# Where layer 1's first operands are loaded inside the expert loop of a two-layer gated cross-attention network

## The reference

```python
x = x + tanh(g_xattn[0]) * L0_xattn(ctx_768, layernorm(x), mask, ...)   # 4 heads of 64, keys: context and x
x = x + tanh(g_ffn[0])   * L0_ffn(layernorm(x), ...)                    # 64 experts, grouped routing
x = x + tanh(g_xattn[1]) * L1_xattn(layernorm(x), ctx_768, ...)         # 16 heads of 64 over 77 keys
x = x + tanh(g_ffn[1])   * L1_ffn(layernorm(x), ...)                    # fake-quantised, 704 wide
```

```python
up   = einsum('td,edh->teh', xt, Wup) + bup
gate = einsum('td,edh->teh', xt, Wgate) + bgate
h    = silu(up) * gate * fs[:, :, None]          # fs: the routing shares
out  = einsum('teh,ehd->td', h, Wdown) + fs @ bdown
```

## Time and profile before

| | us |
|---|---|
| Median of 3 runs | 2242.48 |
| Lowest and highest | 2239.87, 2250.66 |
| The profiled execution | 2242.07 |
| Its span (first to last instruction) | 2240.00 |
| PE busy, x14922 | 2029.5 (91%) |
| DVE busy | 1682.1 (75%) |
| ACT busy | 1221.4 (55%) |
| POOL busy | 661.8 (30%) |

### The profile page before, as it was taken

How to read it: one execution, slowest core, us unless ns; L and a number is a source line. 1 busy time by engine, 2 the same in 40 slices (tenths; PEclk the granted TensorE clock), 3 DMA queues, 4 the chain that set the end, 5 groups by cost and what they waited for, 6 DMA issues and landing times.

```text
span 2240.0 us, 39247 instructions
## 1 busy us (share of the span) xinstructions
PE 2029.5 (91%) x14922; PEld 1248.5 (56%) x14922; DVE 1682.1 (75%) x2822; ACT 1221.4 (55%) x2885; POOL 661.8 (30%) x520
## 2 busy tenths in 40 slices
PE   7797889888977899999989999999999988899896
PEld 3454555555545444444456666666666656676643
DVE  5888686776879889977067777777778867676697
ACT  2455876858855666555523333333333367677585
POOL 0305877868767542000000000000000013243353
PEclk6898999999987999999999999999999999999997
DMA  4232000000000466454586666766766670000002
GB/s 120 70 107 61 1 2 1 2 1 3 21 20 1 164 228 240 200 216 175 210 237 197 203 190 200 205 189 195 205 190 204 192 212 16 1 1 2 1 1 75
DMA packets 134331, 255.34 MB, mean 114 GB/s; under 512 B 17868, under 2 KB 62785, under 8 KB 134017
## 3 DMA queue, kind: packets, MB, share of 16 engines
q1 hardware_dynamic: 113616, 185.05, 27.5%
q10 hardware_dynamic: 20529, 67.79, 7.7%
HBM read 169.28 MB, written 82.44 MB: 112 GB/s over the span
## 4 chain that ended last, share of the span: by engine, by line
PE 59%; DVE 21%; ACT 11%; POOL 4%; issue 3%; DMA 1%; SPq 1%; ACTq 0%; DVEq 0%; POOLq 0%
PE ps L519 56%; DVE arena L1042 8%; DVE arena L1051 6%; ACT arena L2006 5%; DVE arena L1045 3%; PE ps L527 3%; ACT arena L1756 3%; DVE arena L1048 2%; POOL arena L2111 2%; POOL arena L2072 1%; ACT arena L2014 1%; DVE arena L1058 1%; SPq L2205 1%; POOL arena L2124 1%; DMA arena<-share_scratch 1%
## 5 line engine op out<-in xcount | busy, mean ns | idle before, releaser
L519 PE MATMUL ps<-arena 128*128 128x512 f16 (+13 forms) x13708 | 1907.4, 297 | 135.1 <-DVE arena L1051 26.5
L519 PEld LDWEIGHTS ps<-arena 128*128 128x128 f16 (+7 forms) x13708 | 1109.9, 102 | 849.3 <-issue 115.6
L1042 DVE TENSOR_TENSOR arena<-arena 128x512 f32<-128x512 f32 (+6 forms) x992 | 715.1, 753 | 145.2 <-ACT arena L1964 92.4
L1756 ACT ACTIVATE arena<-ps,arena 128x512 f32<-128x512 f32 (+3 forms) x512 | 342.3, 686 | 178.0 <-PE ps L519 161.8
L1042 DVE TENSOR_TENSOR arena<-ps,arena 128x512 f16<-128x512 f32 (+11 forms) x440 | 238.8, 568 | 240.4 <-ACT arena L1760 87.2
L2072 POOL TENSOR_TENSOR arena<-arena 128x4 f32<-128x4 f32 (+5 forms) x51 | 85.2, 1672 | 1084.4 <-DVE arena L1045 1083.9
L1964 ACT CAST arena<-arena 128x512 f16<-128x512 f32 x256 | 158.2, 618 | 436.7 <-DVE arena L1042 432.2
L2111 POOL TENSOR_TENSOR arena<-arena 128x512 f16<-128x512 f32 (+1 forms) x288 | 350.8, 1240 | 65.0 <-ACT arena L1756 63.5
L1756 ACT ACTIVATE arena<-ps 128x512 f16<-128x512 f32 (+1 forms) x512 | 275.2, 611 | 89.2 <-PE ps L519 85.1
L1051 DVE TENSOR_REDUCE arena<-ps 128x1 f32<-128x1024 f32 (+5 forms) x246 | 224.5, 919 | 45.7 <-PE ps L519 42.9
L527 PE MATMUL ps<-arena 128*128 128x128 f32 (+4 forms) x1214 | 192.1, 286 | 70.7 <-DVE arena L1042 26.8
(11 more groups left out here) (81 smaller groups left out, 451.7 us busy)
## 6 DMA issues: line engine op xcount, KB each, us to landing
wide_scratch<-arena ACTq DMA_DIRECT2D x128, 512.0 KB, 2.6
arena<-share_scratch SPq DMA_DIRECT2D x512, 128.0 KB, 3.7
arena<-wide_scratch SPq DMA_DIRECT2D x128, 512.0 KB, 4.8
mq_scratch<-arena SPq DMA_DIRECT2D x16, 308.0 KB
vw_scratch<-arena SPq DMA_DIRECT2D x32, 154.0 KB
arena<-mq_scratch SPq DMA_DIRECT2D x16, 308.0 KB, 5.6
arena<-vw_scratch SPq DMA_DIRECT2D x8, 576.0 KB, 6.4
arena<-in_x SPq DMA_DIRECT2D x4, 1024.0 KB, 9.8
```

The lines of the kernel that those rows point to most:

```text
L519: return e.matmul(o, l, r, start=start, stop=stop, skip_group_check=True)
L1042: return e.tensor_tensor(o, a, b, op)
L1756: return e.activation(o, i, f, bias=bias, scale=scale)
```

## The change

The eight loads of `load1(0)` are no longer issued in a row in the pass of unit 10. `load1` gets an index and issues one load; the pass of unit 128 issues the first, those of units 136, 144, ... 184 the others, each behind the unit's share loads (and reloads, of which an even unit has none). The order of the eight is the same: 308, 308, 576 and 40 KB, and the same again. The waits for `fl` and `st` move along to unit 128. Batches 1 to 3 are loaded after the loop as before, all eight in a row.

```diff
-        def load1(b):
-            for n in range(2):
-                for k in range(2):
-                    load("op%d" % b, MQ[b][:, n, k, :], MQD[n, k, :, b, :])
+        def load1(b, i):
+            n, k = divmod(i, 4)
+            if k < 2:
+                load("op%d" % b, MQ[b][:, n, k, :], MQD[n, k, :, b, :])
+            elif k == 2:
                 load("op%d" % b, VW[b][:, n, 0:9, :], VWD[n, b, 0:1152, :].rearrange("(c p) d -> p c d", p=128))
+            else:
                 load("op%d" % b, VW[b][0:80, n, 9, :], VWD[n, b, 1152:1232, :])
...
-            if n == 10:
+            if n == 128:
                 W.wait_ge("fl", 8)
                 for z in range(3):
                     W.wait_ge("st%d" % z, 256)
-                load1(0)
+            if n >= 128 and n % 8 == 0 and n < 192:
+                load1(0, (n - 128) // 8)
...
         for b in range(1, 4):
-            load1(b)
+            for i in range(8):
+                load1(b, i)
```

## The result

| | before | after |
|---|---|---|
| Median, us (20 runs each) | 2241.64 | 2234.44 |
| Lowest and highest | 2232.36, 2253.62 | 2224.38, 2245.23 |
| Ratio after to before | | 0.9963, 95% interval 0.9947 to 0.9980 |
| The profiled execution | 2242.07 | 2245.03 |
| Its span | 2240.00 | 2243.3 |

What follows compares the result with a forecast made beforehand. TensorE (PE) was taken to bound the kernel, busy 91% of the span. Profiled 2242.07 us, less 7.7 for the burst leaving unit 10, plus 0 for the single loads and 0 for the moved waits, gave 2234.4 us; range 2229.5 to 2242.

Steps and rivals of the forecast that it cites:

- PE's gap, and the chain through SP's eight issues: At units 10 to 12, eight SP issues delay unit 11's shares; DVE waits 6.98 us, PE's gap is 5.74 us.
- Rival A: Unit 11's stall is the loop's start-up and comes back elsewhere: 2242.1 us; chance 0.07 with its partial return.
- rival B: At units 128 to 184 a piece holds the next odd unit's shares over 3.5 us: 2245.0 to 2259.4 us; chance 0.05.
- The price, 7.7 us: At units 10 to 16, PE loses 7.7 us to the burst, bounds 5.74 and 8.4 us, not made up later.
- PE takes 1.2 us of DVE lateness: In the expert loop, PE takes 1.2 us of DVE lateness without a gap, except right after a norm.
- The single loads at 0: Eight single loads at units 128 to 184 cost 0, with an upper end of 10.6 us.
- The 2.3 us in hand: An odd unit's second share load has 6.0 us until needed, landing takes 3.7 median, so 2.3 us are in hand.
- no other issue is moved: On SP's queue at units 128 to 184, free for 2.0 us, a load's 0.45 us issue delays nothing: 0.
- the price of short rows: A couple of 576 and 40 KB takes 2.8 us, the upper end taken for the 576 KB piece.
- the two holds: The burst holds up unit 11 twice: by SP's time to issue it and by the bytes ahead on the same queue.
- fixed cost of 2 us a DMA: If the skill page's fixed cost of about 2 us per DMA blocked the queue, eight pieces would add 16 us.
- Rival C: Stages behind the loop start 7.7 us earlier and get back 3.3 us of clock: 2231.1 us; chance 0.09.

Runs made afterwards that it cites:

- the burst at 112: Changed kernel with all eight loads in a row beside unit 112 instead of spread out; loop 683.98 us, 6.75 over the changed kernel's.
- the burst at 128: Changed kernel with all eight loads in a row beside unit 128; loop 682.54 us, median 2239.17 us, ratio to before 0.9995.
- the halves: Changed kernel with loads 0 to 3 in a row beside unit 116 and 4 to 7 beside unit 172; loop 680.72 us, 3.49 over.
- the burst at 168: Changed kernel with four 308 KB loads in a row at unit 112, 576, 40, 576, 40 KB (512-byte rows) at 168; loop 682.30 us, 5.07 over.
- the loads from unit 16: Changed kernel with its single loads beside every eighth unit from 16 to 72; loop 677.23 us, median 2230.6 us, ratio to before 0.9958.
- the long rows at unit 10: Kernel before, all eight loads in a row at unit 10, with the 576 KB loads in rows of 4608 bytes; loop 682.93 us, 5.70 over the changed kernel's.
- the couples: Changed kernel with two loads at a time: 576 and 40 KB beside units 112 and 120, 308 KB couples beside 176 and 184; loop 677.23 us.

## Why the prediction was right

**The spot and the mechanism.** The step "PE's gap, and the chain through SP's eight issues" was right: the gap, DVE's wait and the dip of the clock are gone after. Rival A is out by the burst at 112 and at 128, rival B by 0.27 us of waiting in all and by the 171.12 us from unit 128 to unit 192. One word of the step was too narrow: it laid the bytes' part to loads ahead "on the same queue". From GpSimd's queue the same bytes still cost 5.20 of the 7.68 us, so most of the price does not hang on the queue.

**The price, 7.7 us.** The loop's length gives 7.68. The two ways of the sum were 7.6 (5.74 of gap and 1.8 of clock) and 7.7 (three pairs at PE's pace). The table bears out the first one elsewhere too: at unit 112, 4.88 us of gap and 1.7 us of clock make 6.6 against 6.75; at unit 168, 3.23 and 1.7 make 4.9 against 5.07. The price belongs to that spot, from whose rows it was worked out: the same burst costs 5.31 us at unit 128 and 6.75 at 112. As the prediction said, the kernel before gives nothing of it back: its Silus are 7.7 us late against the changed kernel from unit 14 to unit 252. Lateness that made no gap of PE is given back elsewhere: behind the four 308 KB loads at 112 the Silus were 0.76 us late at unit 114 and on time again at unit 124. Two small slips stand in the numbers: with a DMA share of 0.67 a pair leaves 1.7 us of DMA time and not 1.8, and the lower bound by its own terms (2231.1 less 2.6) is 2228.5 and not 2229.5. Neither changes anything that was concluded.

**PE takes 1.2 us of DVE lateness.** This came from one row pair (6.98 and 5.74). It held where PE set the pace and at the start of the loop: 6.12 and 4.88, 5.41 and 4.18, 2.80 and 1.57, 2.39 and 1.16, 2.96 and 1.73 each differ by 1.23 or 1.24 us. It is not a constant of the whole loop. At unit 169, where DVE was still catching up, it was 1.09 and 1.08; at unit 129, with the sum of a group around the wait, 1.96.

**The single loads at 0.** Right: the stretch with the loads took as long as without them (171.12 us), and every spread-out placing gave the same loop within 0.05 us. The 2.3 us in hand were enough for a couple: 576 + 40 KB in one go brought no wait. That "no other issue is moved" was not quite so: behind the first 576 KB load SP's next reload took 1.85 us (at 1517.89) instead of 0.58. What was mis-sized is the step of the price of short rows in a longer row of issues. By its rate (2.8 us a couple, 2.0 us passing before the next shares, 2.3 us in hand) two couples would make DVE wait 1.3 us; they made it wait 4.32. It did no harm, as no two 576 KB loads stand together in the change. Where the prediction called SP's time to issue and the bytes ahead the two holds, the part of the bytes turned out the larger at 2464 KB, and SP's time with short rows the larger at 1232 KB.
By the line-rate figure of the Trainium skill ("DMA: Bandwidth & Descriptors", Specifications) rows of 512 B should run as fast as longer ones. The runs here differ from that: the same 1152 KB cost the loop 5.07 us in rows of 512 bytes and 1.50 us in rows of 4608, and the measurement decides. The rate of the DMA engines differs less: with all eight in a row at unit 10 they moved 305 GB/s at a share of 0.99 with long rows (1149 to 1163), and 284 at 1.03 in the kernel before (1145 to 1160).
The fixed cost of 2 us a DMA that the prediction took from the Trainium skill ("DMA: Bandwidth & Descriptors", Anatomy) stands in a section on loads issued by GpSimd, and these are issued by SP. No such cost was added here by the eight single loads.

**What the single loads would do to the neighbours.** The longest landing of a share load rose from 6.1 to 7.3 us; its median from 1450 to 1620 us rose from 3.7 to 4.0, as the prediction had it. The first 576 KB load did bring the one short wait, at unit 146. Unit 145, for which the prediction counted on the norm's extra 1.4 us, had none; but with a load beside every pair the 576 KB loads stood at units 132 and 140, with no norm there, and brought no wait either, so the extra time was not needed.

**The whole time.** 2234.4 forecast and 2234.44 measured. That they agree to a tenth is luck of the scatter, since single runs of the same kernel lie 20 us apart; the loop's 7.68 us is the firm number. Rival C looked for up to 3.3 us of clock given back behind the loop. There after took 435.9 us to its end and before 437.6; over all twelve profiles it is 435.7 to 439.2, so one pair of executions can't show whether the change had a part in it. What C left out is larger and lies ahead of the loop: 12.7 us against the change in these two executions, in stages that the change does not touch.

## What to carry to other kernels

Background loads that nobody needs soon still compete with the small loads that somebody needs in the next microseconds; look for the longest run of issues between two of these, weigh the length of its rows and the time that its issues take as well as its bytes, and cut it to what the consumer has in hand (here 616 KB at a time was free, and 1232 KB with short rows in it was not). Where a kernel's runs scatter by more than a change is worth, compare the length of the stage that it touches: here that repeats within 0.05 us while the whole scatters by 20. A neighbour engine's lateness is free up to some amount, which one pair of rows (its wait and the bound engine's gap) tells for the place where it was taken: here 1.23 us in most places, 1.08 to 1.96 in others.

## What was not expected of the hardware

The length of a gap alone does not tell what the clock takes. A gap of 2.07 us was followed by the longest dip of all, six microseconds at 0.50 (the burst at 128), while 1.94 us (the burst from GpSimd's queue) and 1.73 us (the halves) were followed by none. In the windows table of the burst at 168, one microsecond each, the dip behind a gap of 3.23 us is over in under four:

```profile
1582.00:1583.00 1.00, 1.00 (x7) 0.63 (x5) 0.94 (x2) 0.16 (x1) 0.00 (x0) 0.61 0.32 100
1583.00:1584.00 1.00, 1.00 (x4) 0.39 (x3) 0.86 (x2) 0.46 (x1) 0.00 (x0) 0.50 0.06 20
1584.00:1585.00 1.00, 1.00 (x4) 0.37 (x3) 0.79 (x2) 0.12 (x1) 0.00 (x0) 0.50 0.58 152
1585.00:1586.00 1.00, 1.00 (x4) 0.37 (x3) 0.47 (x1) 1.00 (x2) 0.00 (x0) 0.68 0.69 145
```

One stretch ahead of the loop, in a stage that no kernel here changes, goes with most of the scatter in when the loop starts. The granted clock from 100 to 150 us was 0.63, 0.64, 0.69 and 0.72 in four of the twelve profiles (after, the loads from unit 16, the long rows at unit 10, the couples), and their loops started at 1130.18, 1128.77, 1122.42 and 1121.46 us. In the other eight it was 0.90 to 0.97, with the start between 1112.64 and 1117.77. What sets it off in one execution and not in the next stays open.
